# An attention and expert kernel on one core: key and query joins moved to VectorE, one norm job per batch, later expert loads, and three-bank exponentials from step 2 on

## The reference

```python
xn = layernorm(x)                                  # x: 4 batches x 1024 rows x 128
q, k, v = heads(xn @ Wq.T), heads(xn @ Wk.T), heads(xn @ Wv.T)      # 16 heads of 8
q, k = q*cos + rot(q)*sin, k*cos + rot(k)*sin      # rotary embedding
attn = softmax(q @ k.T * 8**-0.5) @ v
gates = softmax(xn @ gate_w + gate_b); two best experts of 8 for each row
h = gelu(xn @ w1[e] + b1[e]); h = gelu(h @ w2[e] + b2[e]); y = h @ w3[e] + b3[e]
out = x + attn + sum of gate * y over the two experts
```

## Time and profile before

| | |
|---|---|
| median of 3 runs | 656.65 us (656.34 to 656.77) |
| profiled execution, its own time | 658.22 us |
| its span, first to last instruction | 656.5 us |
| PE busy | 620.1 us (94%) |
| ACT busy | 554.6 us (84%) |
| DVE busy | 240.2 us (37%) |
| POOL busy | 217.6 us (33%) |
| mean granted TensorE clock | 0.996 |

### The profile page before, as it was taken

How to read it: one execution, slowest core, us unless ns; L and a number is a source line. 1 busy time by engine, 2 the same in 40 slices (tenths; PEclk the granted TensorE clock), 3 DMA queues, 4 the chain that set the end, 5 groups by cost and what they waited for, 6 DMA issues and landing times.

```text
span 656.5 us, 12557 instructions
## 1 busy us (share of the span) xinstructions
PE 620.1 (94%) x4240; PEld 272.4 (41%) x4240; DVE 240.2 (37%) x696; ACT 554.6 (84%) x575; POOL 217.6 (33%) x235
## 2 busy tenths in 40 slices
PE   9899999989999999899999999999999999999995
PEld 6323332222322222223888888883222222222221
DVE  5664235574232223013555555550122021212204
ACT  3799999999999999898554555559999999999994
POOL 2610003152687767541122122123333323233210
PEclk9999999999999999999999999999999999999999
DMA  7645502442445444875233333210212121122104
GB/s 221 193 161 191 194 33 72 169 144 95 141 145 190 161 148 161 262 210 113 66 72 79 73 73 81 70 56 32 76 53 69 41 69 56 56 68 60 64 17 132
DMA packets 86124, 71.72 MB, mean 109 GB/s; under 512 B 47681, under 2 KB 61793, under 8 KB 86081
## 3 DMA queue, kind: packets, MB, share of 16 engines
q1 hardware_dynamic: 79392, 56.92, 28.8%
q0 software_dynamic: 5968, 13.51, 6.1%
q10 hardware_dynamic: 720, 0.71, 0.5%
HBM read 33.51 MB, written 33.42 MB: 102 GB/s over the span
## 4 chain that ended last, share of the span: by engine, by line
PE 58%; ACT 22%; issue 14%; DMA 2%; DVE 2%; POOL 1%; SPq 1%; ACTq 1%; DVEq 0%; POOLq 0%
ACT probs L654 18%; PE ps L1348 12%; PE ps L1284 10%; PE ps L1332 8%; PE ps L1261 7%; PE ps L1294 5%; PE ps L1277 5%; ACT probs L629 4%; PE ps L1246 3%; PE ps L1209 2%; PE ps L1173 2%; PE ps L1270 1%; PE ps L1167 1%; PE ps L1183 1%; DMA b_raw<-in_L_ffn_b_dram 1%
## 5 line engine op out<-in xcount | busy, mean ns | idle before, releaser
L654 ACT ACTIVATE probs<-ps 128x1536 f32<-128x1536 f32 (+1 forms) x264 | 349.6, 1437 | 8.7 <-PE ps L1332 7.6
L1348 PE MATMUL ps<-probs,v_st 128*32 128x512 f32 x1536 | 208.0, 608 | 3.1 <-DVE v_st L776 1.9
L1332 PE MATMUL ps<-q_st,k_st 32*128 32x512 f32 x768 | 132.8, 495 | 16.5 <-ACT probs L654 11.6
L1332 PEld LDWEIGHTS ps<-q_st,k_st 32*128 32x128 f32 x768 | 49.8, 181 | 197.8 <-ACT probs L654 141.9
L629 ACT ACTIVATE probs<-ps 128x1024 f32<-128x1024 f32 x128 | 121.6, 1035 | 7.2 <-PE ps L1246 5.2
L666 ACT ACTIVATE work<-ps,work 128x256 f32<-128x256 f32 x156 | 70.7, 474 | 65.6 <-PE ps L1284 65.1
L567 POOL DMA_INDIRECT work<-slots_y_d,slot_i x64 | 60.4, 944 | 121.3 <-PE ps L1348 78.0
L528 POOL DMA_INDIRECT slots_x_d<-xn_all,slot_i x64 | 62.1, 971 | 56.6 <-PE ps L1348 32.2
L1261 PE MATMUL ps<-probs,v_st 128*32 128x512 f32 x512 | 70.1, 604 | 6.7 <-ACT probs L629 3.9
L1284 PE MATMUL ps<-work 128*128 128x256 f32 x312 | 73.9, 380 | 0.1
L550 POOL DMA_DIRECT2D slots_y_d<-work x39 | 27.9, 714 | 120.1 <-DVE work L998 115.6
(11 more groups left out here) (152 smaller groups left out, 435.3 us busy)
## 6 DMA issues: line engine op xcount, KB each, us to landing
k_d<-parts SPq DMA_DIRECT2D x8, 1024.0 KB
q_d<-parts SPq DMA_DIRECT2D x8, 1024.0 KB
q_st<-q_d SPq DMA_DIRECT2D x30, 256.0 KB
k_st<-k_d SPq DMA_DIRECT2D x30, 256.0 KB
slots_x_d<-parts SPq DMA_DIRECT2D x5, 1024.0 KB, 7.0
work<-slots_x_d SPq DMA_DIRECT2D x80, 64.0 KB, 2.2
slots_y_d<-work POOLq DMA_DIRECT2D x39, 128.0 KB, 2.2
work<-work SPq DMA_DIRECT2D x24, 128.0 KB
```

What stands on the lines that cost most here:

```text
L654: nc.scalar.activation(group_probs(phase, g)[:, 0:size, :], group_slot(g)[:, 0:size * HALF].rearrange("p (h n) -> p h n", n=HALF), ACT.Exp ...
L1332: ins = nc.tensor.matmul(group_slot(g)[:, n * HALF:(n + 1) * HALF], k_st[32 * h:32 * h + ROWS, mt * P:(mt + 1) * P], q_st[32 * h:32 * h + ...
L1348: ins = nc.tensor.matmul(o_ps[32 * h:32 * h + 32, :], v_st[:, mt, h, :], group_probs(phase, half * HALF_GROUPS + g)[:, n, :], start=(mt == ...
```

## The change

Steps 2 and 3 take the group form too. DVE makes all of a join, in three stages at three blocks in a row. The squares of the third and fourth part of a batch go to a part of `attn_all` that is not yet in use, and one norm job for each batch replaces two. The places of the plain pieces, joins, routing pieces and scatters are written out anew, and the expert loads stand at blocks 13 and 14 of step 7 where they stood at 11, 13 and 15.

```diff
-GROUPED = 4
+GROUPED = 2
-    fixed = {0: ("values", 0, 2), 7: ("norm", 0), 16: ("norm", 1), 50: ("norm", 2), 62: ("norm", 3), 52: ("count",),
+    fixed = {0: ("values", 0, 2), 7: ("norm", 0), 62: ("norm", 1), 94: ("norm", 2), 126: ("norm", 3), 54: ("count",),
...
-    for g, places in enumerate(((36, 38, 41), (39, 42, 45), (46, 51, 54), (53, 55, 58)), 4):
+    for g, places in enumerate(((37, 38, 42), (40, 42, 46), (45, 46, 50), (50, 53, 57),
+                                (64, 66, 70), (70, 72, 76), (74, 78, 82), (80, 86, 90),
+                                (88, 96, 100), (102, 104, 108), (106, 110, 114), (112, 114, 118)), 4):
         for part in range(2):
-            place(("plain", g, part), places[part])
+            fixed[places[part]] = ("plain", g, part)
         joins[places[2]] = g
-    for g in range(8, 16):
-        n = FIRST_JOIN + JOIN_EVERY * (g - 8)
...
-ROUTE_EXP = (2, 5)
+ROUTE_EXP = (2, 7)
...
+    return {FIRST_SCATTER + 9 * i // 4: i for i in range(TILES)}
...
-EXPERT_LOADS = tuple(BLOCKS * (SPLIT - 2) + n for n in (11, 13, 15, 18, 19, 20, 21, 22))
+EXPERT_LOADS = tuple(BLOCKS * (SPLIT - 2) + n for n in (13, 14, 17, 18, 19, 20, 21, 22))
...
-                    if (t, j) in JOINS:
-                        rotate(JOINS[(t, j)])
-                        low_part(JOINS[(t, j)])
-                        square(JOINS[(t, j)])
...
-            def join_parts(g):
+            def join_parts(g, stage):
                 u = g % 2
-                dve.wait_ge(exchanged[u], 32 * (g // 2 - 1))
-                dve.wait_ge(parts_stored[g % 4], 16 * (g // 4))
-                nc.vector.tensor_tensor(high(g), t_cos[:, u, :], t_sin[:, u, :], ALU.add).then_inc(hi_made[u], 1)
+                if stage == 0:
+                    dve.wait_ge(exchanged[u], 32 * (g // 2 - 1))
+                    nc.vector.tensor_tensor(rot[:, u, :], t_cos[:, u, :], t_sin[:, u, :], ALU.add).then_inc(rot_made[u], 1)
+                    dve.wait_ge(parts_stored[g % 4], 16 * (g // 4))
+                    dve.wait_ge(rot_made[u], g // 2 + 1)
+                    nc.vector.tensor_copy(high(g), rot[:, u, :]).then_inc(hi_made[u], 1)
+                elif stage == 1:
+                    dve.wait_ge(hi_made[u], g // 2 + 1)
+                    nc.vector.tensor_tensor(low(g), rot[:, u, :], high(g).bitcast(F32), ALU.subtract).then_inc(lo_made[u], 1)
+                    nc.vector.tensor_copy(high(g, 1), high(g)).then_inc(again_made[u], 1)
+                else:
+                    dve.wait_ge(S["aux_done"], AUX[("norm", g // 4 - 1)] + 1)
+                    nc.vector.tensor_tensor(square_of(g), rot[:, u, :], rot[:, u, :], ALU.mult).then_inc(sq_made[u], 1)
...
-                for u in range(2):
-                    pe.wait_ge(sq_made[u], pair + 1)
-                    ins = nc.tensor.matmul(aux_ps[32 * u:32 * u + 32, :], head_r[:], squares[:, u, :], start=True, stop=True)
+                pe.wait_ge(sq_made[0], 2 * b + 2)
+                pe.wait_ge(sq_made[1], 2 * b + 2)
+                for k in range(4):
+                    ins = nc.tensor.matmul(aux_ps[32 * k:32 * k + 32, :], head_r[:], square_of(k), start=True, stop=True)
```

More of the change, by code:

```diff
@@ L58 @@
 WARM_LATE = (3, 1)
-FIRST_JOIN, JOIN_EVERY = 70, 7
+FIRST_SCATTER = 66
 def heads_of(g):
@@ L132 @@
 AUX = {job: n for n, job in enumerate([JOBS[p] for p in sorted(JOBS)] + [("turn", SPLIT - 1, 1)])}
-ROUTE_EXP = (2, 5)
-ROUTE = {divmod(block, BLOCKS): n for n, block in enumerate((35, 40, 41, 43, 44, 47, 48, 49, 50, 54, 56, 57, 59, 60, 61, 63, 64, 66, 67))}
+ROUTE_EXP = (2, 7)
+ROUTE = {divmod(block, BLOCKS): n for n, block in enumerate((35, 40, 41, 43, 47, 49, 51, 52, 53, 54, 55, 56, 58, 60, 61, 62, 63, 65, 66))}
 def plan_scatter():
[L139 to L143, removed]
-EXPERT_LOADS = tuple(BLOCKS * (SPLIT - 2) + n for n in (11, 13, 15, 18, 19, 20, 21, 22))
+    return {FIRST_SCATTER + 9 * i // 4: i for i in range(TILES)}
+EXPERT_LOADS = tuple(BLOCKS * (SPLIT - 2) + n for n in (13, 14, 17, 18, 19, 20, 21, 22))
 STAGED = (11, 13)
@@ L225, in high, with square_of @@
             return parts[:, g % 4, (0, (1, 2)[g % 2])[copy], :]
+        def square_of(g):
+            if g % 4 < 2:
+                return squares[:, g % 4, :]
+            return attn_all[:, STEPS - 8 + 2 * (g % 4):STEPS - 6 + 2 * (g % 4)].rearrange("p t k c -> p (t k c)")
         def low(g):
@@ L502, in square @@
                 pool.wait_ge(rot_made[u], g // 2 + 1)
-                if g >= 2:
-                    pool.wait_ge(S["aux_done"], AUX[("norm", g // 2 - 1)] + 1)
-                nc.gpsimd.tensor_tensor(squares[:, u, :], rot[:, u, :], rot[:, u, :], ALU.mult).then_inc(sq_made[u], 1)
+                nc.gpsimd.tensor_tensor(square_of(g), rot[:, u, :], rot[:, u, :], ALU.mult).then_inc(sq_made[u], 1)
             pool.wait_ge(S["proj_read"], 1)
@@ L620, in _, with attention_exps @@
             high_part(2)
-            def attention_exps(t, lo=0, hi=UNITS):
-                for u in range(lo, hi):
+            def attention_exps(t):
+                for u in range(UNITS):
                     j, pair = divmod(u, 2)
@@ L631, in attention_exps @@
                                          ACT.Exp, scale=SCALE).then_inc(S["exp_done"], 1)
[L633 to L639, removed]
+            with act.Fori(0, GROUPED) as t:
                 attention_exps(t)
@@ L642, in group_exps @@
                 for g in range(GROUPS):
+                    if isinstance(t, int) and (t, g) == ROUTE_EXP:
+                        act.wait_ge(S["max_made"], 1)
+                        nc.scalar.activation(rt[:, 1], rt[:, 0], ACT.Exp).then_inc(S["exp_made"], 1)
                     act.wait_ge(S["scores_done"], group_units(t) + (g + 1))
@@ L797, in _, with peak @@
                 gate_logits(0, n, v0_ps[n]).then_inc(S["v0_read"], 1)
[L799 to L803, removed]
+            def peak(b):
+                dve.wait_ge(S["aux_done"], AUX[("norm", b)] + 1)
+                nc.vector.tensor_reduce(peaks[:, b:b + 1], aux_ps, AX.X, ALU.max).then_inc(S["aux_read"], 1)
             def prepare_rows(b):
@@ L1029, in _ @@
                         load_v(t + 1, 0)
-                    if (t, j) in JOINS:
-                        join_parts(JOINS[(t, j)])
+                    for stage in range(3):
+                        g = JOINS.get(divmod(t * BLOCKS + j - stage, BLOCKS))
+                        if g is not None:
+                            join_parts(g, stage)
                     if (t, j) in ((0, 11), (1, 3)):
@@ L1222, in turn_bound @@
                 free_aux(AUX[("bound",)])
-                pe.wait_ge(S["bound_made"], 1)
                 for b in range(B):
-                    ins = nc.tensor.matmul(aux_ps[0:1, 64 * b:64 * b + 64], tops[:, b:b + 1], ident[0:64, 0:64], start=True, stop=True)
+                    ins = nc.tensor.matmul(aux_ps[0:1, P * b:P * b + P], peaks[:, b:b + 1], ident, start=True, stop=True)
                 ins.then_inc(S["aux_done"], 1)
```

38 lines of the change are left out of this document (12 added, 26 removed).

## The result

| | before | changed |
|---|---|---|
| median of 12 executions | 656.55 us (654.75 to 659.62) | 653.76 us (652.74 to 657.62) |
| ratio to before | | 0.9957, 95% interval 0.9939 to 0.9975 |
| profiled execution, its own time | 658.22 us | 655.11 us |
| its span | 656.5 us | 653.3 us |
| mean granted clock | 0.996 | 0.995 |

The change wins 2.8 us (0.4%), where 7.65 were forecast; 653.76 lies outside the range of 645.3 to 652.9.

A forecast was written before the change was run, and what follows sets the result against it. ACT's floor of 28.81 us a group step was taken to bound, plus PE pieces beyond each cycle's slack and a key stop before step 8. Changes of steps 1 to 8 summed to -7.65 us: 649.0 us, range 645.3 to 652.9.

The forecast's parts named there:

- Are the keys there?: Start of step 8: its key load, issued ahead of the expert loads, lands in time, with a margin of 2 us.
- Rival (3): The stop before step 8 stays or second halves come late; 3.66 us of gain lost, 652.7 us; chance 0.12.
- I take it off the median: Whole kernel: the saving of 7.65 us, read in the profiled execution, is subtracted from the median of 656.65 us.
- Fit by less, about 0.5. I charge nothing: Step 3's start: part 5's stage 1 and a routing piece fit ahead of DVE's copy by about 0.5 us; no cost.
- rival (4): DVE late for the copy of `o_ps` or the pieces' bank, 0.3 us in each of twelve parts; 652.6 us; chance 0.08.
- The joins on DVE: Twelve parts: at most 3.2 us of DVE each for 0.69 before, hidden in its idle time and charged nothing.
- The scatters: DVE's 24 added copies could hold POOL's indirect DMAs by 0.56 us, which their spacing takes up; no change in the sum.
- Step 2: Group form wins nothing, as ACT's shorter work meets a full PE; 31.9 us for 31.56, +0.3.
- Step 1: Loses a norm of 0.84 us in pair form; taken as -0.2 us, bounds 0 and -0.84.
- Rival (5): DVE's join delays cost more than the change wins, at 1 us for a part 661 us; chance 0.05.
- The cycles: Each step grows by what PE's pieces exceed the slack of their own cycle, 0.64, 0.05 or 0.3 us.
- rival (2): PE's pieces count by their plain sum per step; steps 2 to 8 save 10.8 us, 645.8 us; chance 0.22.

The follow-up runs named there:

- experiment 1: Changed kernel with the stores of parts 9 and 13 issued one block later, behind the loads of the second halves of steps 5 and 7; 651.4 us.
- experiment 3: Changed kernel with the stores of parts 9 and 13 one block earlier, at block 14, ahead of the next part's exchange; 651.15 us.
- experiment 4: Changed kernel with the store of part 11 issued at block 0 of step 6, right ahead of the second-half key loads; 655.53 us.
- experiment 5: Kernel of experiment 4 with that store and the second-half loads of step 6 held further, for the second group of scores; 657.8 us.
- experiment 6: Kernel before with only the expert loads moved, to blocks 13, 14 and 17 for 11, 13 and 15 in step 7; 653.02 us.
- experiment 10: Changed kernel, stores of parts 9 and 13 at block 14, one routing piece moved from block 15 of step 2 to block 0 of step 3; 650.07 us.
- experiment 7: Kernel before with only the joins changed, made by DVE alone in three stages; 656.47 us.
- experiment 11: Kernel of experiment 10 with step 3's two plain pieces of part 7 and count moved to blocks 0, 6 and 8; 649.3 us.
- experiment 9: Kernel of experiment 1 with the norms of steps 3, 5 and 7 moved from block 14 to block 13, with values; 652.64 us.
- experiment 8: Changed kernel with the pair form kept in steps 2 and 3, 653.52 us; the same with stores of parts 9 and 13 at block 14, 651.06 us.

## Why the prediction was wrong

**The step that failed.** It asked for the keys of step 8 only: "Are the keys there?" was answered for one load, and the loads of the other steps were put at nothing. The change gives eleven of the twelve stores another place in SP's queue. Those of parts 9 and 13 came to stand at block 15 of steps 4 and 6, between an exchange that waits for g = 20 and the loads at block 0, and this new order was not read against those loads. The runs showed two stops there, of 1.72 and 0.95 us of PE. They cost 2.4 us of the median, and moving the two stores one block either way takes them off (experiments 1 and 3). Experiments 4 and 5 say in one profiled execution each that lateness and bytes are both needed. Rival (3) named such a stop, the second halves among its causes. Its 652.7 is near the result by luck: it placed the stop at step 8, where there was none, and its price, 3.66 for 2.4, made up in part for the mistake in the base that follows.

**The base of the sum.** "I take it off the median" was the second mistake, about as large. From the profile of before to that of experiment 1, which is the change without its stops, the time falls by 7.5 us (658.22 to 650.72), close to the 7.65 of the forecast. The median falls by 5.2 (656.55 to 651.4). The profiled execution of before was 1.6 us above its median and that of experiment 1 0.7 under its own. With the 2.4 us of the stops these 2.3 make up the 4.8 us between forecast and result.

What the profiled execution of before had more than the others stays open in part. The low clock behind its stop is not it: of the 54 executions of this kernel that ran beside the experiments, 49 had a mean clock of 0.996 or less (this one has 0.996) and took 654.8 to 660.6 us, and the five above took 654.4 to 655.1. In experiments 1, 3 and 6, which have no stop, 14 of 17 executions have 0.997 or more. So most executions of before have such a stretch, and its 1.53 us stood in the sum rightly. A part is plain scatter: experiment 6 has the same code up to step 7, and in its profile steps 3, 5 and 6 take 31.80, 30.91 and 31.16 us, 0.9 less in sum than in the earlier trace rows.

**DVE late for the copy.** "Fit by less, about 0.5. I charge nothing" was the join of part 5 at step 3. It cost 0.73 us of PE, 0.8 in the step (experiment 10). This is rival (4), at one place of twelve.

**What held.** The joins on DVE had the prices given (0.68, 0.43, 0.69, 0.42, 0.69 us) and were neutral in sum (experiment 7). The scatters did not suffer: an indirect DMA took 0.97 us in the mean before and after. Step 2 won nothing with the group form: 31.91 for 31.9. Step 1 fell by 0.30 us for 0.2. The keys of step 8 came in time, worth what was said (experiment 6: step 7 2.5 less, step 8 2.25). Rival (5) did not come.

**The cycles.** Here rival (2), the plain sum, was the better rule for three steps, and I had called it the less likely. Without the stops (experiment 1) steps 4, 5 and 6 take 30.41, 29.48 and 29.75 us; its sum says 30.4, 29.5 and 29.8, my cycles 30.7, 29.85 and 30.1. PE is busy for the whole of these three windows. Step 7 lies between the two (29.66; sum 28.9, cycles 30.15), step 2 is as the cycles have it (31.9 for 31.7 by the sum), and step 8 (29.38) is 0.5 above both. For the norm the reason is visible. I charged 0.7 at g = 20, and in the trace it costs its 1.00 us of PE:

```profile
149.06 0.62 PE L1172 MATMUL ps<-squares,head_r 128*32 128x512 f32 x2
149.08 0.62 PE L1172 MATMUL ps<-attn_all,head_r 128*32 128x512 f32 x2
...
150.06 0.50 PE L1320 MATMUL ps<-q_st,k_st 32*128 32x512 f32 x3
```

but where no values are issued ACT hardly waits for it. Steps 4 and 6 have no norm, so this does not explain them. The place of a piece still counts, as the plain sum denies: a plain piece in a place with values costs 0.26 us more than one without (experiment 11), a norm 0.34 to 0.44 in its own step, waits apart, of which up to 0.2 comes back in the next (experiment 9). Steps 2 to 8 without the stops come to 211.9 us for 212.5 forecast. That they agree so well is partly luck, steps 4 to 7 forecast 0.3 to 0.5 too high against steps 3 and 8 0.4 and 0.5 too low.

**The sum again,** in medians: 656.55, less 3.5 for the expert loads (experiment 6), less 1.6 for the pieces' and norms' new places, the joins and the form together (experiment 6 to experiment 1, 653.02 to 651.4, not taken apart further), plus 2.4 for the two new stops: 653.8. Each term is a difference of two medians, and the kernel before itself ran at 656.55 to 656.9 beside them, so each is good to some tenths.

## What to carry to other kernels

In a DMA queue issued in order, the place of a transfer is not its time: it leaves when the last wait ahead of it is released. When entries are moved, go through each load that an engine needs soon, and add what the wait ahead of it takes and what bytes go out just before it; either alone may fit the margin where both do not. Take a saving off the execution in which it was read, or read it in more than one: here the profiled execution was 1.6 us above the median of its kernel.

## What the runs showed of the hardware

**A wait of PE and the clock.** After some waits of PE the granted clock fell to the lower level for about 3.4 us, and after others of the same length it did not. It fell after 2.65 us (before, 0.54 over 3.66 us), after 1.72 (the changed kernel, 0.55 over 3.80 us) and after 1.59 (step 3 of experiment 8, 0.95 over the step). It did not fall after 2.1 us in the profiled execution of experiment 7, nor after 1.42 in step 6 of experiment 5. In step 5 of experiment 4 the wait is 1.70 us and the clock stays at 1.00:

```profile
180.88:212.15 31.27, 29.57 (x218) 8.54 (x220) 12.05 (x27) 29.42 (x23) 13.46 (x14) 1.00 0.44 151
```

against 32.79 us in the changed kernel and 29.48 in experiment 1. So this stop costs 1.8 us and, with the low clock, 1.5 more. In the profile of experiment 5 the clock after the same wait was low for twice as long (0.51 over 7.0 us), and step 5 took 34.29 us. Of the twelve executions of the changed kernel the four with a mean clock of 0.995 or less took 654.8 to 657.6 us, the eight others 652.7 to 654.4.

**Scatter.** The versions in whose profile PE has no wait for keys spread least, 0.3 us (649.15 to 649.44 in four executions of the best) to 2.3; those with one spread by 3.3 to 7.6 us (653.74 to 661.29 in ten of experiment 5).

**A load behind a store.** A key load of 256 KB landed after 5.4 to 5.8 us right behind a 1 MB store on the same queue, after 4.4 us where the store went out 3.5 us ahead (experiment 3), and after 3.0 us with the store behind it (experiment 1).

By the Trainium skill, "SBUF — State Buffer", section "SBUF: two separate sides", DVE and GpSimd lock each other out of a shared port pair. The trace agrees in so far as no copy to `v_st` takes over 0.46 us in steps 2 to 8 of the changed kernel, where POOL's `tensor_tensor` is gone, against 1.82 before. Nothing measurable was won by it in experiment 7, where the joins move in the same way.
